# A decoder's transformer stack on one core: half 1's norm and quantisation one slot earlier, and ScalarE copying two of three turned blocks

## The reference

```python
x = x + _L1_attn_ref(_layernorm(x), w_project, w_out)          # causal, 16 heads
x = x + _L1_xattn_ref(_layernorm(x), ctx, ...)                 # 8 groups x 2 heads of 128
# in _L1_xattn_ref:
ln_out = _ln(hidden_states, ln_w, ln_b)
q = _ln(_fp8_linear(ln_out, wq, ...));  k = _ln(_fp8_linear(ln_out, wk, ...));  v = _fp8_linear(ln_out, wv, ...)
core = _gqa(q, k, v)
qx = _ln(_fp8_linear(ln_out, wqx, ...));  kx, vx = split(ctx @ w_kv_x);  xout = _gqa(qx, _ln(kx), vx)
catq = _div_clamp_fp8(concatenate([core, xout]), proj_smooth)
return (catq @ wproj) * scales
```

## Time and profile before

| | |
|---|---|
| time, median of 3 runs | 998.78 us (998.55 to 1000.34) |
| the profiled execution's own time | 998.71 us |
| its span, first to last instruction | 996.9 us |
| mean granted TensorE clock | 0.966 |
| busy: TensorE, VectorE, ScalarE, GpSimd | 911.4, 713.1, 563.8, 150.5 us |
| weight loads of TensorE | 681.3 us |
| DMA, all queues | 56.80 MB |

### The profile page before, as it was taken

The page is one execution under the profiler, slowest core; times in us unless marked ns, Lnnn a source line. Parts: engine busy times, 40 slices in busy tenths (PEclk is TensorE's granted clock), DMA queues, the critical chain, the costliest instruction groups (busy, mean ns, idle before and its releaser), DMA issues.

```text
span 996.9 us, 15862 instructions
## 1 busy us (share of the span) xinstructions
PE 911.4 (91%) x5254; PEld 681.3 (68%) x5254; DVE 713.1 (72%) x1549; ACT 563.8 (57%) x2101; POOL 150.5 (15%) x194
## 2 busy tenths in 40 slices
PE   5989999998879679999999999999999998789796
PEld 3647566656558567888888787878787776545453
DVE  3674545666686886887888788888888787765653
ACT  3461335446345856777877676877777776321311
POOL 2001202000033331121212111121212121000000
PEclk9999999999889879999999999999999999889898
DMA  7001000000101312232432432423422623110000
GB/s 218 1 23 42 0 1 1 2 1 1 43 1 43 85 43 55 73 94 71 113 94 55 112 81 59 129 54 75 117 70 54 198 57 78 47 43 0 22 0 21
DMA packets 64083, 56.80 MB, mean 57 GB/s; under 512 B 11201, under 2 KB 62978, under 8 KB 64002
## 3 DMA queue, kind: packets, MB, share of 16 engines
q1 hardware_dynamic: 63904, 55.76, 20.7%
q10 hardware_dynamic: 98, 0.03, 0.0%
HBM read 21.15 MB, written 1.05 MB: 22 GB/s over the span
## 4 chain that ended last, share of the span: by engine, by line
PE 43%; DVE 24%; SPq 18%; issue 5%; DMA 5%; ACT 4%; POOL 2%; DVEq 0%; ACTq 0%
SPq L548 18%; DVE laid L1676 6%; PE ps L956 6%; DMA group_probsT<-laid 4%; PE ps L876 4%; PE ps L835 3%; DVE group_probs L1670 3%; PE ps L889 3%; PE ps L692 2%; PE ps L682 2%; PE ps L904 2%; PE ps L705 2%; DVE neg_max L1575 2%; PE ps L850 2%; PE ps L744 2%
## 5 line engine op out<-in xcount | busy, mean ns | idle before, releaser
L1258 ACT ACTIVATE group_probs<-ps,score_bias 128x256 f32<-128x256 f32 x256 | 117.2, 484 | 55.9 <-DVE score_bias L1659 55.9
L835 PE MATMUL ps<-group_w_hi,xq 128*128 128x256 f32 (+1 forms) x512 | 133.4, 301 | 5.5 <-POOL xq L1995 5.5
L1659 DVE TENSOR_REDUCE score_bias<-ps 128x2 f32<-128x512 f32 x128 | 87.7, 691 | 59.8 <-PE ps L889 59.8
L876 PE MATMUL ps<-group_probsT,group_values 128*128 128x512 f32 x256 | 120.8, 608 | 5.1 <-DVE x_all L1683 3.0
L835 PE MATMUL ps<-group_w_lo,xq 128*128 128x256 f32 (+1 forms) x512 | 122.9, 282 | 0.0
L1215 ACT ACTIVATE group_squares<-ps 128x128 f32<-128x128 f32 x384 | 108.7, 340 | 16.4 <-PE ps L835 9.2
L889 PE MATMUL ps<-group_kT,group_qT 128*128 128x256 f32 x512 | 115.9, 379 | 0.0
L889 PEld LDWEIGHTS ps<-group_kT,group_qT 128*128 128x128 f32 x512 | 97.0, 190 | 26.6 <-issue 10.5
L835 PEld LDWEIGHTS ps<-group_w_hi,xq 128*128 128x128 f32 x512 | 100.1, 196 | 7.1 <-issue 5.6
L835 PEld LDWEIGHTS ps<-group_w_lo,xq 128*128 128x128 f32 x512 | 100.0, 195 | 1.0
L1215 ACT ACTIVATION_READ_ACCUMULATOR group_squares<-ps 128x1 f32 x384 | 97.5, 274 | 0.0
(11 more groups left out here) (258 smaller groups left out, 1775.3 us busy)
## 6 DMA issues: line engine op xcount, KB each, us to landing
group_probsT<-laid SPq DMA_DIRECT2D x512, 64.0 KB, 2.1
group_raw_p<-in_L_xattn_wproj_dram SPq DMA_DIRECT2D x16, 256.0 KB, 3.4
group_raw_w<-in_L_xattn_wq_dram SPq DMA_DIRECT2D x8, 256.0 KB, 2.8
group_raw_w<-in_L_xattn_wqx_dram SPq DMA_DIRECT2D x8, 256.0 KB, 3.0
group_raw_w<-in_L_xattn_w_kv_x_dram SPq DMA_DIRECT2D x16, 128.0 KB, 3.2
x_all<-in_x_dram SPq DMA_DIRECT2D x2, 512.0 KB, 6.0
front_work<-in_ctx_dram SPq DMA_DIRECT2D x1, 1024.0 KB, 6.6
group_raw_w<-in_L_xattn_wk_dram SPq DMA_DIRECT2D x8, 128.0 KB, 3.2
```

The costliest lines, as they stand in the source:

```text
L835: last = pe.matmul(c.ps[:, bank, at:at + width], x_, w[:, k, col:col + width], start=k == 0 and m == 0, stop=k == KD - 1 and m == 1)
L876: last = pe.matmul(c.ps[:, bank, :].rearrange("p (i n) -> p i n", i=BLOCKS), c.values[:, item % 4, kt, side, :], c.probsT[item % 2][:, kt, ...
L1258: last = act.activation(c.probs[:, side, h, t, :], c.ps[:, fills.bank(name), t * S:(t + 1) * S], ACT.Exp, bias=c.score_bias[:, i:i + 1], a ...
L1659: v.tensor_reduce(c.score_bias[:, i:i + 2], c.ps[:, bank, :].rearrange("p (t n) -> p t n", n=S), AX.X, ALU.max, negate=True).then_inc(nega ...
```

## The change

In the causal steps ScalarE copies blocks 0 and 1 of the turned probabilities and VectorE block 2 alone. Block 1 of step i-1 is copied between the two pairs of exponentials of step i. `heads_out(0)` comes behind the average of its round. In round 11 the inversion of step 9's sums is left to round 12. ScalarE takes half 0's tokens and scales kind 0 in round 13, and VectorE clamps kind 0 later in that round.

In the slots half 1's chain comes earlier: `heads_out(1)` between the two token tiles of slot 0, its add and Q1's statistics between the two normalisations of slot 0, norms Q1 and Q2 at the start of slot 1, the turned tokens and kinds 0 and 1 in slot 1, kinds 2 and 3 in slot 2. In slots 1 to 3 VectorE takes the weights ahead of the laying. GpSimd's order follows. The weights of slot 0 use banks 6, 7, 6 instead of 5, 6, 7. The diff, cut to its core:

```diff
@@ plan_slot
-    for i, (g, w) in enumerate(o.weights):
-        f.plan(W_BANKS[i], ("W", g, w))
+    for (g, w), bank in zip(o.weights, (6, 7, 6) if o.n == 0 else W_BANKS):
+        f.plan(bank, ("W", g, w))
...
-    if o.n == 2:
+    if o.n == 1:
         f.plan(4, ("xT", "Q", 1, 0))
         f.plan(7, ("xT", "Q", 1, 1))
@@ tensor, visit
                     if o.projects:
                         project_item(o, 0)
-                    if o.weights:
+                    if o.n == 0:
+                        next_weights(o, slice(0, 2))
+                        heads_out(1)
+                    elif o.weights:
                         next_weights(o)
                     if o.turns_first:
                         turn_item_heads(o)
                     if o.projects:
                         project_item(o, 1)
+                    if o.n == 0:
+                        next_weights(o, slice(2, 3))
                     if o.outputs:
                         output_item(o)
-                    if o.n == 0:
-                        heads_out(1)
...
-                    if o.n == 2:
+                    if o.n == 1:
                         turn_tokens("Q", 1, twice[1], normed_count("Q2"))
@@ tensor, steps
-                    if i == OUT_STEP:
-                        heads_out(0)
                     for w in FIRST_STEPS.get(i, ()):
                         first_weights(w)
                     if 0 <= i - 1 < STEPS:
                         average(i - 1)
+                    if i == OUT_STEP:
+                        heads_out(0)
@@ scalar, visit
                     if o.n == 0:
                         take_projection(o, 0)
-                        next_weights(o)
+                        next_weights(o, slice(0, 2))
                         take_projection(o, 1)
+                        next_weights(o, slice(2, 3))
                         return
...
-                    if o.n == 2:
+                    if o.n == 1:
                         take_affine(1)
                         scale_kind(1, 0)
                         scale_kind(1, 1)
-                    if o.n == 3:
+                    if o.n == 2:
                         scale_kind(1, 2)
                         scale_kind(1, 3)
@@ scalar, steps
                     if i < STEPS:
                         exps(i, 0)
+                    if i == QUANT_STEP + 1:
+                        take_affine(0)
+                    if i >= 1:
+                        take_probs(i - 1, 1)
+                    if i < STEPS:
                         exps(i, 1)
-                        take_probs(i)
+                        take_probs(i, 0)
+                    if i == QUANT_STEP + 1:
+                        scale_kind(0, 0)
...
-                    if i == QUANT_STEP:
-                        take_affine(0)
-                    if i + 1 in QUANTISED:
+                    if i + 1 in QUANTISED and i > QUANT_STEP:
                         scale_kind(0, QUANTISED[i + 1])
@@ vector, visit
+                    if o.n == 0:
+                        next_weights(o, slice(0, 2))
+                        normalise_item(o, (0,))
+                        add("Yc", 1)
+                        take_moments("Q1", 1, x[1])
+                        normalise_item(o, (1,))
+                        next_weights(o, slice(2, 3))
+                        return
+                    if o.n == 1:
+                        normalise("Q1", 1, x[1], xn[1], None)
+                        take_moments("Q2", 1, xn[1])
                     if o.turns:
                         invert_sums(o, 0)
                     if o.outputs:
                         quantise_item(o)
+                    if o.n < 4:
+                        next_weights(o)
+                    if o.n == 1:
+                        normalise("Q2", 1, xn[1], twice[1], normed[1])
                     if o.turns:
                         lay_item_probs(o, 0)
                         invert_sums(o, 1)
-                    if o.weights:
+                    if o.weights and o.n >= 4:
                         next_weights(o)
                     if o.turns:
                         lay_item_probs(o, 1)
                     if o.outputs:
                         add_item(o)
-                    if o.n == 1:
-                        normalise("Q1", 1, x[1], xn[1], None)
-                        take_moments("Q2", 1, xn[1])
                     if o.projects:
                         normalise_item(o)
-                    if o.n == 0:
-                        add("Yc", 1)
-                        take_moments("Q1", 1, x[1])
-                    if o.n in (2, 3):
-                        clamp(1, 2 * o.n - 4)
-                        round_kind(1, 2 * o.n - 4)
+                    if o.n == 2:
+                        clamp(1, 2)
+                        round_kind(1, 2)
                     if o.scores:
                         item_max(o, 0)
                         item_max(o, 1)
                     if o.n == 1:
-                        normalise("Q2", 1, xn[1], twice[1], normed[1])
-                    if o.n in (2, 3):
-                        clamp(1, 2 * o.n - 3)
-                        round_kind(1, 2 * o.n - 3)
+                        clamp(1, 0)
+                        round_kind(1, 0)
+                        clamp(1, 1)
+                        round_kind(1, 1)
+                    if o.n == 2:
+                        clamp(1, 3)
+                        round_kind(1, 3)
@@ vector, steps
-                    if 0 <= i - 1 < STEPS:
-                        take_probs(i - 1, 1)
                     if i == STEPS:
-                        take_probs(i - 1, 2)
-                    if i in QUANTISED:
+                        take_probs(i - 1)
+                    if i in QUANTISED and i > QUANT_STEP + 1:
                         clamp(0, QUANTISED[i])
...
-                        if i % 2 and i < STEPS - 1:
+                        if i % 2 and i < STEPS - 1 and i != OUT_STEP + 1:
                             invert_heads(i - 2)
                         elif i % 2 == 0 and i < STEPS:
+                            if i == OUT_STEP + 2:
+                                invert_heads(i - 3)
                             take_heads(i - 3)
...
+                    if i == QUANT_STEP + 1:
+                        clamp(0, QUANTISED[i])
@@ gpsimd
-                visit(SLOTS[0])
+                head_scale(SLOTS[0], 0)
                 root_of("Q1", 1)
+                head_scale(SLOTS[0], 1)
                 root_of("Q2", 1)
-                visit(SLOTS[1])
-                for o in SLOTS[2:4]:
-                    visit(o)
-                    split(1, 2 * o.n - 4)
-                    split(1, 2 * o.n - 3)
+                head_scale(SLOTS[1], 0)
+                head_scale(SLOTS[1], 1)
+                split(1, 0)
+                head_scale(SLOTS[2], 0)
+                split(1, 1)
+                head_scale(SLOTS[2], 1)
+                split(1, 2)
+                head_scale(SLOTS[3], 0)
+                split(1, 3)
+                head_scale(SLOTS[3], 1)
```

More of the change, by code:

```diff
@@ L810, in first_weights, with next_weights @@
                     turn_weight(("W", 0, w), w)
-                def next_weights(o):
-                    for g, w in o.weights:
+                def next_weights(o, which=slice(None)):
+                    for g, w in o.weights[which]:
                         if w == 6:
@@ L1576, in row_max, with take_probs @@
                                         negate=True).then_inc(lowered, 1)
-                def take_probs(i, m):
-                    if i >= 2 and m == 1:
+                def take_probs(i):
+                    if i >= 2:
                         if i % 2:
@@ L1583, in take_probs @@
                             v.wait_ge(averaged, (i - 2) // 2 + 1)
-                    name = ("P", i, m)
+                    name = ("P", i, 2)
                     bank = fills.wait_full(v, name)
-                    fills.drain(v.tensor_copy(pT[i % 2][:, m, :], c.ps[:, bank, :]), name)
+                    fills.drain(v.tensor_copy(pT[i % 2][:, 2, :], c.ps[:, bank, :]), name)
                 def invert_heads(i):
@@ L1633, in take_weight, with next_weights, normalise_item @@
                     fills.drain(last, name)
-                def next_weights(o):
-                    for g, w in o.weights:
+                def next_weights(o, which=slice(None)):
+                    for g, w in o.weights[which]:
                         take_weight(("W", g, w), w, g)
-                def normalise_item(o):
-                    for t in range(2):
+                def normalise_item(o, tiles=(0, 1)):
+                    for t in tiles:
                         v.wait_ge(rstd_ready, 2 * o.n + t + 1)
```

13 lines of the change are left out of this document (5 added, 8 removed).

## The result

| | before | after |
|---|---|---|
| median of the runs beside each other | 1000.52 us (9 runs, 995.48 to 1004.65) | 994.17 us (9 runs, 992.56 to 997.95) |
| the profiled execution's own time | 998.71 us | 993.24 us |
| its span, clock | 996.9 us, 0.966 | 991.4 us, 0.963 |

The ratio is 0.9937, 95% interval 0.9914 to 0.9959: about 6.3 us faster, where 12.4 were forecast, and outside the range (992.5). Measured once more beside its variants it was 0.9952 (0.9937 to 0.9966).

A forecast was written before the change was run, and what follows sets the result against it. TensorE was taken as the bound, full from 386 to 860 us, not before. Step 4 -1.1, copies +0.8, steps 10 to 16 -4.0, slots 0 to 2 +2.1, slot 3 -3.2, slot 4 -7.0: -12.4, 986.3 us, range 981.0 to 992.5.

The forecast's parts named there:

- Step 4's wait: Causal step 4: TensorE's 1.13 us wait goes, since ScalarE now copies block 1 and isn't behind the norm; -1.1 us.
- the ring of copies: Causal steps: scores, exponentials, turn and copy over two engines; +0.1 us in 8 steps, +0.8; as rival "Slower" 0.06, 1003.5 us.
- Steps 10 to 12: Causal steps up to the tokens' turn: the norm and the turn behind it come 2.2 us earlier; -2.2 us.
- Slot 4: Slot 4: kinds 2 and 3 split a slot ahead, so waits for `xq` and slow projections behind them go; -7.0 us.
- Steps 12 to 16: Steps behind the tokens: scores' wait -2.0, VectorE's copies -2.0, later exponentials +0.6, a held clamp +1.6; sum -1.8 us.
- Slots 0 to 2: Half 1's chain one slot earlier: VectorE's kinds and hold +2.0, GpSimd's roots +1.1, tokens' turn out of slot 2 (1.0); +2.1 us.
- the lead is eaten in slots 1 and 2: Rival, chance 0.17: VectorE's two kinds before item 0's laying take the steps' 4.0 and slot 3's 3.2 us; 991.4 us.
- Slot 3: Slot 3: `wp_lo` comes before the laying instead of at 349.17; -3.2 us.
- The port: VectorE and GpSimd exclude each other for a whole instruction; holds cost 1.6 us in the steps, 3.6 in the slots.
- its rival without holds: Rival, chance 0.10: splits fall where VectorE works from PSUM, three new holds go, 5.2 us; 981.1 us.
- SP's moves: Rival, chance 0.10: 16 moves an item become the bound, the lead shrinks to 8 us instead of 12; 990.4 us.

The follow-up runs named there:

- GpSimd's order alone: The changed kernel with one edit: GpSimd's scale of slot 0's second head tile in front of the root of Q1; ratio 0.9914 to the kernel before.
- slots-alone run: The kernel before with the slots as changed and the causal steps left as before; ratio 0.9967 to the kernel before.
- tokens later: The changed kernel with half 0's tokens turned in round 13 behind the scores, ScalarE's affine step behind its exponentials; ratio 0.9857 to the kernel before.
- yardstick: The changed kernel itself, measured once more beside its variants on their chip; ratio 0.9952 to the kernel before.
- both edits: The changed kernel with VectorE's weights first in slots 0 and 1, GpSimd's Q1 root behind the head scale, and tokens later; 0.9812 of the kernel before, 981.7 us.
- weights first: The changed kernel with VectorE's weights ahead of slot 0's second normalisation and norm Q1, GpSimd's Q1 root behind the head scale; 0.9877 of the kernel before.
- clamps late: The changed kernel with clamp and mask of kinds 1 and 2 behind the row maxima and copy of their round; ratio 0.9922 to the kernel before.

## Why the prediction was wrong

**Right.** Step 4's wait of 1.13 us went, and the slow products behind it, and the ring of copies cost nothing that the trace shows: scores waited for exponentials 1.59 and 0.24 us, at 166 and 206 us, where they waited 1.58 and 0.23 before. The +0.8 for it was not needed. Steps 10 to 12 brought 2.4 for 2.2. Slot 4 brought 6.4 for 7.0: the wait for `xq` and the slow stretch behind it. The sign was right.

**Steps 12 to 16: -1.8 forecast, +2.0 measured.** The failed step is what stands behind "TensorE will then stand waiting for it about 3 us". The wait was sized rightly (2.94) and counted as the bound of the tokens' start, but what comes after it was put at nothing: the level of 1.2 GHz until 276.4 us, for the tokens' turn, a step's scores, an average and the turns of five blocks. Elsewhere the same sum had counted such slow products as a gain where a wait went (0.8 us in step 12, 2.7 in slot 4). VectorE waited 6.29 us, until 269.40, for the masks of step 14's first scores (5.15 in a run with a short low clock, GpSimd's order alone), and clamps, copies and splits stand behind that. From the tokens' turn to slot 0's last kind the clock was at its lower level for 16.6 us, against 7.2 before.

How much of the miss is the clock can be read from the run with GpSimd's order alone, the same instructions up to there. It had 6.8 us of low clock in this stretch, and the stretch took 30.1 us, against 32.8 in the changed kernel and 30.8 before. So of the 3.8 us by which the term missed, some 2.7 go with the clock. The other 1.1 stay at a clock no worse than before: TensorE's waits in the stretch came to 7.9 us there, against 8.0 before, although the term took off 2.0 for the scores' wait and 2.0 for VectorE's copies. The scores' wait went down to 0.56, and an average stood 2.67 us for VectorE's copy of block 2 instead. What makes that copy late is open.

That the wait brings the long low clock isn't shown for each execution. Behind the 2.9 us wait it lasted 10 to 14 us in five profiles of this order and 3.4 in two, and the slots-alone run had long low clocks around its tokens without this wait. What is shown is the place of the turn: with the wait filled with work that was ready (tokens later), the stretch from step 10 to the last kind took 43.9, 44.9 and 44.5 us in three profiles, against 49.3 to 52.0 in six of the changed kernel's steps, and the run's ratio is clear of the yardstick's. At the same 6.8 us of low clock (both edits, GpSimd's order alone) 44.9 stand against 49.3, so 4.4 us go with the turn's place and with ScalarE's affine step, which moved with it; how they divide isn't shown. The wait itself fell by 2.3, and scores then waited 2.6 for ScalarE.

The Trainium skill (TensorE: Matmul & The Clock Gate, section "Part 1: The HAM clock gate (the "warmup" mystery)") says that the clock depends on how busy TensorE has been recently, and that the count of slow products differs from run to run. The trace agrees with the second, by the 3.4 us and the 10 to 14 us behind the same wait. To the first it gives no simple tie: TensorE was busy 13.13 of 13.24 us at a granted clock of 0.50.

**Slots 0 to 2: +2.1 forecast, +5.5 measured.** The failed step is this term, mis-sized by 3.4 us. It counted VectorE's work in slots 1 and 2 and "GpSimd's roots in front of the heads' scale". It did not follow what `heads_out(1)` in the middle of slot 0 puts last: the second projection, its squares, the head scale, and on VectorE behind the second normalisation the low part of a weight, and in slot 1 behind norm Q1 and its statistics another one. PSUM banks for slot 1's weights and turned heads are not free before these. The chain on VectorE in the changed kernel:

```profile
308.45 1.02 DVE L1654 TENSOR_TENSOR group_heads<-ps,head_rstd 128x384 f32<-128x384 f32 x2 [3.00 <-POOL head_rstd L2006]
309.38 0.60 DVE L1635 SCALAR_TENSOR_TENSOR group_w_lo<-ps,w_scale,group_w_hi 128x128 fp32r<-128x128 f32 x2
309.90 1.37 DVE L1427 TENSOR_SCALAR second<-x_all,half_mv,half_rstd 128x256 f32<-128x256 f32 x4
311.31 1.41 DVE L1419 BATCH_NORM_STATS2 half_stats<-second 128x6 f32<-128x256 f32 x4
312.75 0.38 DVE L1422 BATCH_NORM_AGGREGATE half_mv<-half_stats 128x2 f32<-128x6 f32 x4
313.05 0.58 DVE L1635 SCALAR_TENSOR_TENSOR group_w_lo<-ps,w_scale,group_w_hi 128x128 fp32r<-128x128 f32 x2
```

Each of the two L1635 rows ends a wait of TensorE: 1.16 us at 310.04 and 1.46 at 313.68. Taking the weights first shortened the stretch to slot 1's scores by 2.7 us, and that to slot 2's scores by 5.3, back to its length before. Of the 2.6 us that are left of the 5.3, 1.0 is the tokens' turn, which used to stand in slot 2, and in that run 1.7 is the wait for norm Q2 in front of it. The rival "the lead is eaten in slots 1 and 2" had put the loss on VectorE's two kinds; slot 2 kept its length (18.4 and 18.5 us) although the turn had left it, so they cost about 1 us (an estimate from these two lengths and the 1.0 of the turn).

**Slot 3: -3.2 forecast, -1.9 measured.** The longest wait for `wp_lo`, in front of slot 3's scores, fell from 4.7 to 1.1 us, as reckoned (the 4.1 that is left is slot 2's, 2.1 before), but ScalarE's exponentials now hold the bank of the weight 2.1 us (1.2 before). The term took the whole of VectorE's lateness for TensorE's.

**The port.** By the Trainium skill (SBUF — State Buffer, "SBUF: two separate sides") a GpSimd instruction and a VectorE instruction of certain kinds exclude each other for the whole of the one that starts first. The trace agrees: five instructions of VectorE were held beside a split between 262 and 400 us, against three before. Four maxima read out of PSUM at 344.21, beside the split at 344.37, took their usual 2.48 us.

```profile
277.36 2.23 DVE L1617 TENSOR_SCALAR front_work<-front_work 128x1024 uint16<-128x1024 uint16 x1
...
332.38 3.03 DVE L1679 TENSOR_SCALAR group_probs<-group_probs,score_inv 128x256 f32<-128x256 f32 x4
```

What that is worth in time isn't shown: the run made to remove them only moved them. The forecast puts the holds at 1.6 us in the steps and 3.6 in the slots; its sum for the slots shows 1.9 only, so the 5.2 us that its rival without holds takes off don't come out of its own terms.

**SP's moves** were given 0.10, with the lead lost after slot 4. In the changed kernel 0.8 us of the lead went by slot 8, while VectorE's laying stood for them 1.6 and 1.4 us. With weights first alone 3.4 went in slot 4; with both edits 0.5 there, against the changed kernel's slot 4. So they stand close behind; whether they are the next bound is not settled.

## What to carry to other kernels

When work is reordered so that TensorE must wait for one long norm, the wait (2.9 us here) is not the whole price: slow products and late copies can follow. Ask what TensorE can do meanwhile, and put the dependent turn behind that. When a product is put in the middle of a slot, follow each PSUM bank behind it to the instruction that frees it, in that engine's own order; small weight copies that free banks go before long norms. A lead won early is worth what the next chain lets through (here perhaps the 16 moves, after which the next laying went on 12.2 to 13.4 us from their first issue), and it is cheaper to look for that chain before than after.

## What the runs showed of the hardware

**Same instructions, 7 us apart.** Eleven profiled executions have the same program up to step 10 (the changed kernel's steps) and reach L705 there between 240.66 and 247.88 us. The early and the late one:

```profile
60.00:100.00 40.00, 37.16 (x154) 25.28 (x153) 22.01 (x48) 14.73 (x27) 2.76 (x4) 1.00 0.13 40
100.00:158.00 58.00, 54.26 (x214) 35.37 (x213) 27.13 (x63) 19.24 (x35) 7.29 (x6) 1.00 0.00 0
158.00:190.00 32.00, 29.68 (x307) 21.24 (x306) 23.61 (x59) 19.27 (x51) 6.52 (x6) 1.00 0.01 2
```

```profile
60.00:100.00 40.00, 37.15 (x140) 25.24 (x139) 20.59 (x43) 13.63 (x26) 2.76 (x4) 0.91 0.13 40
100.00:158.00 58.00, 54.26 (x201) 35.63 (x200) 28.20 (x65) 18.46 (x36) 7.28 (x6) 1.00 0.00 1
158.00:190.00 32.00, 30.17 (x254) 21.24 (x252) 18.01 (x48) 17.31 (x43) 6.46 (x6) 0.89 0.00 1
```

(windows of the run with both edits, then of tokens later). The difference is the granted clock around 60 to 100 us and 158 to 190 us. It goes with single profiles that lie some us apart, and is why the lengths of stretches are compared above, not times from the start. The lengths vary with the clock too: step 10 to slot 0's last kind took 49.3 to 52.0 us in six profiles of the same instructions, and 52.4 and 57.1 in two of the steps before. Why one execution is granted more isn't seen in the trace.

**Length of the low clock.** The same 2.94 us wait at the same place was followed by 10 to 14 us of low clock in five profiles (to about 275 us in the yardstick and to 276 in the changed kernel's first profile) or by 3.4 in two (clamps late and GpSimd's order alone, which have the same order up to there). In the long ones the fall begins inside the wait or some 2 us behind it. How long it lasts was not settled.
